# The bias of V on TensorE by a row of ones, V read straight from PSUM, and a new order of V and U in a decoder layer's prologue

## The reference

```python
input_norm = norm(hidden, axis=-1)              # hidden = layernorm(x)
scaled = hidden / (input_norm + 1e-09)
q  = scaled @ Wq.T + bq
v  = scaled @ Wv.T + bv
tq = q @ anomaly_matrix
scores = q @ tq.T / sqrt(256)
ctx = softmax(scores) @ v * input_norm
```

## Time and profile before

| what | value |
|---|---|
| median of 3 runs | 826.67 us (826.08 to 827.56) |
| profiled execution | 824.5 us, its span 822.3 us |
| TensorE busy (matmuls) | 753.7 us, 92% of the span |
| TensorE's weight loads | 668.3 us, 81% |
| VectorE busy | 629.5 us, 77% |
| ScalarE busy | 456.1 us, 55% |
| mean granted TensorE clock | 0.968 |

### The profile page before, as it was taken

How to read it: one execution, slowest core, us unless ns; L and a number is a source line. 1 busy time by engine, 2 the same in 40 slices (tenths; PEclk the granted TensorE clock), 3 DMA queues, 4 the chain that set the end, 5 groups by cost and what they waited for, 6 DMA issues and landing times. The chain is left out here.

```text
span 822.3 us, 19916 instructions
## 1 busy us (share of the span) xinstructions
PE 753.7 (92%) x6231; PEld 668.3 (81%) x6232; DVE 629.5 (77%) x1614; ACT 456.1 (55%) x924; POOL 165.8 (20%) x255
## 2 busy tenths in 40 slices
PE   4867978999999999999999999999997769999996
PEld 4766867888888888888888888888896658999996
DVE  5782835798888988889889898898886855777773
ACT  2444625766666666666666666666664712443342
POOL 3110022203123032130320312303122011222221
PEclk9888989999999999999999999999999969999999
DMA  6044074133131231321313303133167281111110
GB/s 218 5 139 142 0 271 141 57 110 108 40 128 67 77 106 38 132 89 49 106 40 130 106 32 111 58 108 106 38 225 305 98 326 28 36 41 39 41 32 16
DMA packets 51147, 80.95 MB, mean 98 GB/s; under 512 B 4894, under 2 KB 29216, under 8 KB 50976
## 3 DMA queue, kind: packets, MB, share of 16 engines
q1 hardware_dynamic: 49232, 75.63, 27.5%
q0 software_dynamic: 1872, 4.76, 1.6%
HBM read 45.60 MB, written 35.18 MB: 98 GB/s over the span
## 5 line engine op out<-in xcount | busy, mean ns | idle before, releaser
L1185 ACT ACTIVATE ps_cross<-flip 128x512 f16<-128x512 f32 (+1 forms) x256 | 124.8, 515 | 104.7 <-PE flip L897 83.5
L1409 DVE TENSOR_TENSOR ps_cross<-flip,ps_cross 128x512 f16<-128x512 f32 (+1 forms) x256 | 145.0, 584 | 29.9 <-ACT ps_cross L1185 29.0
L1370 ACT ACTIVATE exp_cross<-exp_cross,xneg 128x1024 f32<-128x1024 f32 (+1 forms) x128 | 122.7, 960 | 27.3 <-DVE xneg L1599 27.3
L897 PE MATMUL flip<-ident,exp_cross 128*128 128x128 f32 (+1 forms) x832 | 130.0, 279 | 6.7 <-DVE ps_cross L1409 3.6
L886 PE MATMUL scores<-keys_cross,qt 128*128 128x402 f32 x512 | 126.4, 369 | 3.6 <-ACT exp_self L1359 1.9
L897 PEld LDWEIGHTS flip<-ident,exp_cross 128*128 128x128 f32 (+1 forms) x832 | 94.0, 141 | 15.1 <-DVE ps_cross L1409 5.1
L739 PE MATMUL scores<-keys_self,u_tile 128*128 128x512 f32 x384 | 102.2, 403 | 4.1 <-issue 2.2
L908 PE MATMUL cross_out<-vals_cross,ps_cross 128*128 128x128 f16 (+1 forms) x832 | 100.7, 222 | 0.3 <-DVE ps_cross L1409 0.2
L910 PE MATMUL cross_out<-vals_cross,ps_cross 128*128 128x64 f16 (+1 forms) x832 | 94.0, 194 | 0.0
L873 PE MATMUL flip<-vals_self,ps_self 128*128 128x256 f16 x768 | 93.7, 276 | 0.0
L908 PEld LDWEIGHTS cross_out<-vals_cross,ps_cross 128*128 128x128 f16 (+1 forms) x832 | 75.4, 100 | 20.9 <-issue 14.7
(11 more groups left out here) (225 smaller groups left out, 1215.8 us busy)
## 6 DMA issues: line engine op xcount, KB each, us to landing
rows_dram<-pads SPq DMA_DIRECT2D x17, 520.0 KB, 4.0
w_piece<-W SPq DMA_DIRECT2D x32, 256.0 KB, 2.9
w_dram<-w_high SPq DMA_DIRECT2D x32, 256.0 KB, 2.3
w_dram<-w_piece SPq DMA_DIRECT2D x32, 256.0 KB, 2.7
w1s<-w_dram SPq DMA_DIRECT2D x8, 1024.0 KB, 12.6
w2s<-w_dram SPq DMA_DIRECT2D x8, 1024.0 KB, 12.5
u_dram<-u_out SPq DMA_DIRECT2D x4, 1024.0 KB, 5.9
u_tile<-u_dram SPq DMA_DIRECT2D x16, 256.0 KB, 2.7
```

The lines of the kernel that those rows point to most:

```text
L897: tr = pe.transpose(flip[0:rows, bank(use), n * P:(n + 1) * P], exp_cross[:, h % 2, m * P:m * P + rows], ident[:, :])
L1185: return act.activation(out, in_, ACT.Copy, **kw)
L1370: act.activation(exp_cross[:, h % 2, cols], exp_cross[:, h % 2, cols], ACT.Exp, bias=xneg[:, h % 2, 1:2], scale=-1.0, accum_out=xden[:, ha ...
L1409: return dve.tensor_tensor(out, full, hi, ALU.subtract)
```

## The change

The bias of V is added on TensorE: each V tile's accumulation starts with two matmuls of a single row (a row of ones times the high and the low part of bv, [1, 256]), then the 6 of before. V's high and low parts are then made straight from PSUM, 512 columns at a time, so v_tmp and the 16 additions go. U goes to scores banks 0 and 1. The bound and the first bias products are earlier in all engines' orders, and so is the wait for the four small loads (bq, bv, bg, Wg). TensorE's order behind mixed product two is: transposes of group 1, bias products, then U(g), V(g+1), transposes of group g+2. On VectorE the low parts of V stand at the head of a group, U's low part stands ahead of the next row scaling, wk_dup's low parts move from group 0 to 1, and those of wv, wq, wo from 1 to 2. The diff, cut:

```diff
+    bv_parts = sb("bv_parts", [1, 2, D], F32R, pro)
+    one_row = sb("one_row", [1, P], F32R, pro)
...
-    pro_v_biased = sem("pro_v_biased")
+    bv_hi = sem("bv_hi")
+    bv_parts_set = sem("bv_parts_set")
...
         for g in range(4):
-            if g == 2:
+            if g == 1:
                 pool.wait_ge(bound_step, 3)
                 pool.tensor_tensor(v_bound[:, 2:3], v_bound[:, 1:2], plus_half[:, 0:1], ALU.pow).then_inc(bound_rooted, 1)
...
             for o in range(C):
                 if g == 0:
                     pe.wait_ge(mixed_lo, 2)
-                    pe.wait_ge(bound_step, 3)
-                    pe.wait_ge(mixed_bias_set, 2)
                 pe.wait_ge(pro_xt_lo, C * (g + 1))
                 if g:
                     pe.wait_ge(u_lo_ready, C * (g - 1) + o + 1)
-                out = self_out if o == 0 else cross_out
-                three(out[:, :], lambda a, c: mixed[:, 1, a, c, o * P:(o + 1) * P],
+                three(scores[:, o, :], lambda a, c: mixed[:, 1, a, c, o * P:(o + 1) * P],
                       lambda b, c: keys_self[:, b, c, g * 512:(g + 1) * 512]).then_inc(pro_u_ready, 1)
...
         tr.then_inc(wq_flipped, 1)
+        pe.wait_ge(bound_step, 2)
+        pe.matmul(scores[:, 3, 0:1], ones[:, :], bound16[:, :], start=True, stop=True).then_inc(bound_summed, 1)
         flip_x_pro(0)
+        pe.wait_ge(biases_loaded, 64)
+        for o in range(C):
+            for c in range(C):
+                mm = pe.matmul(cross_out[:, 8 + o:9 + o], w_raw[:, 2, c, o * P:(o + 1) * P], bq_col[:, c:c + 1],
+                               start=(c == 0), stop=(c == C - 1))
+        mm.then_inc(bias_mixed, 1)
         pe.wait_ge(self_w_lo, 2)
...
             for n in range(4):
                 if g == 0:
                     pe.wait_ge(self_w_lo, 3)
+                    pe.wait_ge(bv_parts_set, 2)
+                    pe.wait_ge(bound_step, 3)
                 pe.wait_ge(pro_xt_lo, C * (g + 1))
                 if g and n % 2 == 0:
-                    pe.wait_ge(pro_v_biased, 4 * (g - 1) + n + 2)
-                three(scores[:, 2 + n // 2, (n % 2) * D:(n % 2 + 1) * D],
-                      lambda a, c: keys_self[:, a, c, (4 * g + n) * P:(4 * g + n + 1) * P],
-                      lambda b, c: w_self[:, 1, b, c, :]).then_inc(pro_v_ready, 1)
+                    pe.wait_ge(pro_v_lo, 2 * (g - 1) + n // 2 + 1)
+                out = scores[:, 2 + n // 2, (n % 2) * D:(n % 2 + 1) * D]
+                for part in range(2):
+                    pe.matmul(out, one_row[:, :], bv_parts[:, part, :], start=(part == 0), stop=False)
+                three(out, lambda a, c: keys_self[:, a, c, (4 * g + n) * P:(4 * g + n + 1) * P],
+                      lambda b, c: w_self[:, 1, b, c, :], first=False).then_inc(pro_v_ready, 1)
...
-        pe.wait_ge(bound_step, 2)
-        pe.matmul(cross_out[:, 0:1], ones[:, :], bound16[:, :], start=True, stop=True).then_inc(bound_summed, 1)
-        pe.wait_ge(biases_loaded, 64)
-        for o in range(C):
-            for c in range(C):
-                mm = pe.matmul(cross_out[:, 8 + o:9 + o], w_raw[:, 2, c, o * P:(o + 1) * P], bq_col[:, c:c + 1],
-                               start=(c == 0), stop=(c == C - 1))
-        mm.then_inc(bias_mixed, 1)
         flip_x_pro(1)
         pe.wait_ge(mixed_bias_set, 1)
-        pe.wait_ge(bound_step, 3)
...
-        self_u(0)
-        for g in range(1, GROUPS):
-            self_v(g)
+        for g in range(GROUPS):
+            self_u(g)
             if g < GROUPS - 1:
-                flip_x_pro(g + 1)
-            self_u(g)
-
+                self_v(g + 1)
+            if g < GROUPS - 2:
+                flip_x_pro(g + 2)
...
                 if g:
                     pe.wait_ge(cross_k_lo, H * (g - 1) + h + 1)
                 elif h < 2:
-                    pe.wait_ge(mixed_lo, 2)
+                    pe.wait_ge(u_lo_ready, C * GROUPS)
                 else:
-                    pe.wait_ge(pro_v_biased, 4 * GROUPS)
+                    pe.wait_ge(pro_v_lo, 2 * GROUPS)
                 three(scores[:, h, 0:KB], lambda a, c: wk_dup[:, a, c, h, :, :],
...
+        def v_hi(g):
+            for n in range(2):
+                act.wait_ge(pro_v_ready, 4 * g + 2 * n + 2)
+                act.wait_ge(self_scale_step, 2)
+                act.activation(vals_self[:, 4 * g + 2 * n:4 * g + 2 * n + 2, 0, :],
+                               scores[:, 2 + n, :].rearrange("p (m d) -> p m d", m=2), ACT.Copy,
+                               scale=self_scale[:, 0:1]).then_inc(pro_v_hi, 1)
+
         xt_hi_pro(0)
+        act.wait_ge(biases_loaded, 64)
+        copy(bv_parts[:, 0, :], bv_row[0:1, :]).then_inc(bv_hi, 1)
         act.wait_ge(mixed_ready, 1)
         copy(mixed[:, 0, 0, :, :], scores[:, 1, :].rearrange("p (c n) -> p c n", c=C)).then_inc(mixed_hi, 1)
+        v_hi(0)
         act.wait_ge(mixed_ready, 2)
         copy(mixed[:, 1, 0, :, :], scores[:, 0, :].rearrange("p (c n) -> p c n", c=C), scale=1.0 / 16.0).then_inc(mixed_hi, 1)
         for g in range(GROUPS):
+            if g:
+                v_hi(g)
             if g < GROUPS - 1:
                 xt_hi_pro(g + 1)
-            for n in range(4):
-                act.wait_ge(pro_v_biased, 4 * g + n + 1)
-                act.wait_ge(self_scale_step, 2)
-                act.activation(vals_self[:, 4 * g + n, 0, :], v_tmp[:, n % 2, :], ACT.Copy,
-                               scale=self_scale[:, 0:1]).then_inc(pro_v_hi, 1)
             u_hi(g)
...
         dve.memset(ctx_t[:, :, :, M:MP].bitcast(F32), 0.0).then_inc(v_scale_step, 1)
+        dve.memset(one_row[:, :].bitcast(F32), 1.0).then_inc(bv_parts_set, 1)
+
+        def v_lo(g):
+            for n in range(2):
+                dve.wait_ge(pro_v_hi, 2 * g + n + 1)
+                dve.scalar_tensor_tensor(out=vals_self[:, 4 * g + 2 * n:4 * g + 2 * n + 2, 1, :],
+                                         in0=scores[:, 2 + n, :].rearrange("p (m d) -> p m d", m=2), scalar=self_scale[:, 0:1],
+                                         in1=vals_self[:, 4 * g + 2 * n:4 * g + 2 * n + 2, 0, :], op0=ALU.mult,
+                                         op1=ALU.subtract).then_inc(pro_v_lo, 1)
+
         statistics_pro(0)
-        statistics_pro(1)
+        dve.wait_ge(self_w_loaded, 48)
+        dve.tensor_tensor_reduce(v_tmp[:, :, :].rearrange("p c n -> p (c n)"), w_raw[:, 1, :, :].rearrange("p c n -> p (c n)"),
+                                 w_raw[:, 1, :, :].rearrange("p c n -> p (c n)"), 1.0, 0.0, ALU.mult, ALU.add,
+                                 v_bound[:, 0:1]).then_inc(bound_step, 1)
+        dve.wait_ge(bound_step, 1)
+        dve.tensor_scalar(bound16[:, :], v_bound[:, 0:1], 1.02, None, ALU.mult).then_inc(bound_step, 1)
         scale_rows(0)
...
+        dve.wait_ge(bound_summed, 1)
+        dve.tensor_copy(v_bound[:, 1:2], scores[:, 3, 0:1]).then_inc(bound_step, 1)
+        dve.wait_ge(biases_loaded, 64)
+        dve.wait_ge(bv_hi, 1)
+        low(bv_parts[:, 1, :], bv_row[0:1, :], bv_parts[:, 0, :].bitcast(F32)).then_inc(bv_parts_set, 1)
+        statistics_pro(1)
+        dve.tensor_reduce(v_bound[:, 3:4], bv_row[:, :], AX.X, ALU.max, apply_absolute_value=True).then_inc(bound_step, 1)
         dve.wait_ge(mixed_hi, 1)
-        dve.tensor_tensor_reduce(v_tmp[:, :, :].rearrange("p c n -> p (c n)"), w_raw[:, 1, :, :].rearrange("p c n -> p (c n)"),
-                                 w_raw[:, 1, :, :].rearrange("p c n -> p (c n)"), 1.0, 0.0, ALU.mult, ALU.add,
-                                 v_bound[:, 0:1]).then_inc(bound_step, 1)
+        dve.wait_ge(bound_step, 4)
+        dve.wait_ge(bound_rooted, 1)
+        dve.tensor_tensor(v_bound[:, 4:5], v_bound[:, 2:3], v_bound[:, 3:4], ALU.add).then_inc(bound_step, 1)
+        dve.wait_ge(bound_step, 5)
+        dve.tensor_scalar(v_bound[:, 5:6], v_bound[:, 4:5], 1e-30, 1.0 / SELF_TOP, ALU.max, ALU.mult).then_inc(bound_step, 1)
+        dve.wait_ge(bound_step, 6)
+        dve.reciprocal(self_scale[:, 0:1], v_bound[:, 5:6]).then_inc(self_scale_step, 1)
+        dve.tensor_scalar(self_scale[:, 1:2], v_bound[:, 5:6], 1.0 / P_TOP, None, ALU.mult).then_inc(self_scale_step, 1)
+        dve.wait_ge(self_scale_step, 2)
+        dve.wait_ge(bias_mixed, 1)
+        dve.tensor_copy(mixed_bias[:, 0, :], cross_out[:, 8:8 + C]).then_inc(mixed_bias_set, 1)
         scale_rows(1)
-        dve.wait_ge(bound_step, 1)
-        dve.tensor_scalar(bound16[:, :], v_bound[:, 0:1], 1.02, None, ALU.mult).then_inc(bound_step, 1)
+        v_lo(0)
...
         for g in range(GROUPS):
+            if g:
+                v_lo(g)
             if g < GROUPS - 1:
                 xt_lo_pro(g + 1)
+            if g == 0:
+                dve.wait_ge(bias_mixed, 2)
+                dve.tensor_scalar(mixed_bias[:, 1, :], cross_out[:, 16:16 + C], 1.0 / 16.0, None, ALU.mult).then_inc(mixed_bias_set, 1)
+                dve.wait_ge(mixed_bias_set, 2)
             if g < GROUPS - 2:
```

(34 more changed lines are left out.)

## The result

The changed kernel takes 831.28 us (median of 20, 824.41 to 833.95) against 826.01 (20, 823.19 to 828.22). The kernel is slower; the forecast was 825.3. The executions also spread wider, 9.5 us against 5.0. The profiled one took 829.99 us, its span 828.2.

The account below looks back on a forecast made before the run. The prediction took a ring of U stores in the prologue, gating cross V, as the bound: a start 3.33 us earlier and a ring 1.98 us longer gave -1.35 us, 825.3 us for the median, range 822.9 to 829.0.

Parts of the forecast that it names:

- V of group 0: TensorE's chain to the ring's start: 24 products at 3.66 us plus the single-row products at 1.6, 5.26 together.
- 8 products of a single row: Bias products inside V of group 0, two per tile: 0.2 us each, 1.6 us in all, ends 1.0 and 2.3.
- rival E: Clock stays low from the start through U of group 0: net +4.6 us, 831.2; chance 0.05.
- My upper end: Highest cost allowed for one single-row product on TensorE: 0.283 us, nothing overlapped; 0.2 was taken.
- the ring's start: End of context piece 0's low part on VectorE: forecast 35.96 against 39.29 before, 3.33 us earlier.
- about 10 us of dense work: Argument against rival E: dense TensorE work from 15.6 us on would not leave the clock low.
- this rule's value: If a single row counted as another tiling mode, draining TensorE: single-row products 2.3 us, ring's start at 36.7.
- The ring: Prologue cycle: context piece's low part, store, U high, U low, VectorE's other work, next low part; 1.98 us longer.
- the three low parts: Low parts of wv, wq, wo on VectorE, between U low and context piece 2: +1.81 us in round 2.
- round 1: Ring from U high's start to context piece 1's low part: 5.59 us against 5.42 before, +0.17.
- Rival B: Clock falls under U of group 0: +2.7 us on the ring's start, net +1.4, 828.0; chance 0.25.
- U of group 3: ScalarE's U high at the ring's end, ahead of cross V: start about 67.0 us against 68.32 before.

Follow-up runs that it names:

- e1: Changed kernel with the bias of V added by two matmuls of 128 rows in place of two of a single row: 825.84 us, ratio 0.9995.
- e7: e1 plus 30 small one-column matmuls at TensorE's start: 824.97 us, ratio 0.9992.
- e8: Changed kernel with 128-row bias matmuls in group 0 only, single rows kept in groups 1 to 3: 825.06 us, ratio 0.9999.
- e12: Same kernel as e1, run once more for one look: 826.59 us.
- e4: Changed kernel with the wait for the four small loads and the first bias products moved behind mixed product one: 825.70 us, ratio 1.0000.
- e3: Changed kernel with the cross weights' low parts ahead of U's low part of groups 1 and 2, in VectorE's waits: 829.02 us, ratio 1.0036.
- e6: Kernel before the change, with SyncE issuing the store of U ahead of the next context load and its wait: 821.56 us, ratio 0.9954.
- e9: Changed kernel with the edits of e1, e3, e4, e6 and e7 together: 811.79 us, ratio 0.9837.
- e2: Changed kernel without the matmuls that add the bias of V, so bv is left out: 822.99 us, ratio 0.9975.

## Why the prediction was wrong

The step that failed is the line "V of group 0" with its "8 products of a single row" in the chain on TensorE, and the weight given to rival E: that step was put at 5.26 us and took 9.07. A second term was missing, the second store's +1.79. The other terms held to within 1 us. Term by term, profile of the changed kernel against the forecast:

- Loads landed, bias products begin: 14.15 against 14.66.
- Bias products and transposes: 1.73 + 0.87 = 2.60 against 1.80; low clock under the first eight.
- Mixed product one: 2.84 against 2.72.
- V of group 0: 9.07 against 5.26, +3.81. Two causes, which e1 and the later groups part. Size: at the full clock two single rows add 1.33 - 0.75 = 0.58 to a tile, 0.29 each, since the six products behind them take 0.90 in place of 0.75. My upper end, 0.283, was about right, and the 0.2 that I took was not; for eight that is 0.7 us. Clock: the remaining 3.1 us, V at 2.30 a tile all through.
- Mixed product two: 2.45 against 1.48, low clock again.
- 16 one-column products 1.71 (1.95), U 2.99 (3.08), then 5.12 to the ring's start (5.01).

Together +4.97: 40.93, not 35.96. This is rival E's mechanism in part, priced there at +5.9 and given 0.05: the clock stayed low through V and mixed product two, but was up again under U of group 0 (2.99), for which E had 2.7 more. That E's 831.2 stands beside the measured 831.28 is luck: it had V at 7.3 in place of 9.07, the low clock under U, and no slow second store. I held "about 10 us of dense work" against it and counted the single rows as dense. e1, e7, e8 and e12 show that with 128 rows my argument holds (V 4.2 to 5.1), and e4 that with single rows the clock can even fall under V. Why the rows matter to the clock is open; the runs show only that they do, and e3 that they don't in every execution.

TensorEngine Tiling (Array Packing), Key Properties, in the Trainium skill, says that changing the tiling mode drains TensorE. The trace agrees as far as a loss of overlap goes: 0.29 for a single-row product and its surroundings against 0.12 for one of 128 rows (e1: 0.94 a tile of eight), with the weight loads of both kinds no longer ahead of their matmuls. Whether a single row counts as another tiling mode no run here shows. I had set this rule's value at the upper end and not taken it.

The ring was right: the three low parts cost 1.78 (1.81), round 1 5.49 (5.59), e3 and e6 confirm it. That its start would come earlier was wrong for this kernel (40.93 after 39.29) and holds only with full rows: 35.58 and 36.20 in e1 and e12 against 35.96. Rival B (the clock falls under U of group 0) did not happen here, U took 2.99; it did in e9, where U took 5.47. The low clock under U of group 3 in some profiles was covered by the store. Missed altogether: the second store, +1.79. It is in e1 too, which has the ring's start as forecast and ends at 0.9995 where the sum gave 0.9984; but 0.9984 lies in e1's interval, and e7, without the slow store, did not come out clearly lower (0.9992), so no run shows that the store explains the difference.

The forecast's 66.97 for U of group 3 and the measured 73.47 differ by 6.50: 4.97 + 1.79 - 0.26 of small terms.

Open: why the part behind the prologue (from the loop's first product to the end) is 722.5 us here, 721.6 before and 723 to 727 in the others, longest in e2 (727.1), whose prologue gave 4.2 us and whose time fell by 2. It hides effects of 1 us. How often V of group 0 gets the full clock in the changed kernel is open too.

## What to carry to other kernels

A matmul that contributes one row is not a small matmul: here it cost more than twice a full one, and the clock was low around it in most executions profiled; give it all 128 rows if the data is there in all of them. Where a single buffer is stored and refilled, write the ring down, and put other work in the wait for the store, not between the last write and the store (0.5% here by the order of two lines on SyncE alone). Added instructions also move later instruction transfers (30 matmuls moved one from 52.93 to 41.49), and a store on the critical chain may meet one.

## What was not expected of the hardware

- Two single-row products of 256 columns and the six full ones behind them: 1.33 us at the full clock, 2.30 at the low one; two full ones and six: 0.94.
- The granted clock fell at 18.1 us in e4, to a mean of 0.51 from 18 to 24 us, while TensorE's busy time was 6.00 of 6.00.
- Single-row and 128-row products side by side: the weight load starts with its matmul (37.07 and 37.50 in the changed kernel), and 0.11 us ahead of it where both have 128 rows (e1).
- A 16 KB instruction transfer some 4 us behind (58.5 against 54.35 in the changed kernel) the issue of a 1 MB store went with 7.9 us to landing, in place of 5.9 to 6.1.
